# An inverse square root seeded on ScalarE by logarithm and exponential, in a windowed-attention transformer

## The reference

```
qkv = shift(x) @ Wqkv                  # 128 -> 3 * 1024
q = q / max(||q||, 1e-12) * q_scale    # per head; the same for k
q, k = rotary(q), rotary(k)            # with a growing / falling scale
sim = 8 * q k^T  in a window of 32 and the one before it
x = softmax(sim) v @ Wo + x
xn = (x' - mean) / sqrt(var + 1e-5) * g + b     # x' = shift(x)
a, gate = split(xn @ W1 + b1)
x = a * gelu(gate) @ W2 + b2 + x
```

## Time and profile before

| | |
|---|---|
| median of 3 runs | 1795.9 us (1795.12 to 1799.96) |
| the profiled execution | 1795.17 us, span 1793.4 us |
| mean granted TensorE clock | 0.965 |
| busy: PE / DVE / ACT / POOL | 1619.5 / 1467.1 / 1106.4 / 992.7 us |

### The profile page before, as it was taken

How to read it: one execution, slowest core, us unless ns; L and a number is a source line. 1 busy time by engine, 2 the same in 40 slices (tenths; PEclk the granted TensorE clock), 3 DMA queues, 4 the chain that set the end, 5 groups by cost and what they waited for, 6 DMA issues and landing times. The chain is left out here.

```text
span 1793.4 us, 75405 instructions
## 1 busy us (share of the span) xinstructions
PE 1619.5 (90%) x31917; PEld 1247.0 (70%) x32013; DVE 1467.1 (82%) x3193; ACT 1106.4 (62%) x1990; POOL 992.7 (55%) x952
## 2 busy tenths in 40 slices
PE   5369999899999889999989999999999989999985
PEld 2147777677777767777767777767777767777762
DVE  8768888888888888888888888888888788888852
ACT  5236666566666656666656666666666656666652
POOL 2246646665555666555666546676556485565420
PEclk8579999999999999999999999999999999999998
DMA  3011111211101210111111111111101111011101
GB/s 100 26 51 36 39 28 31 77 32 36 50 24 36 61 46 27 47 36 36 56 42 38 47 36 35 52 46 39 47 24 39 59 47 39 24 47 39 36 14 48
DMA packets 40597, 74.95 MB, mean 42 GB/s; under 512 B 8992, under 2 KB 22088, under 8 KB 40264
## 3 DMA queue, kind: packets, MB, share of 16 engines
q1 hardware_dynamic: 40264, 70.11, 13.3%
HBM read 20.08 MB, written 2.10 MB: 12 GB/s over the span
## 5 line engine op out<-in xcount | busy, mean ns | idle before, releaser
L773 POOL TENSOR_TENSOR qk<-qk,qk_sin 128x512 f32<-128x512 f32 x384 | 490.9, 1278 | 217.0 <-DVE qk_sin L847 217.0
L781 POOL TENSOR_TENSOR qk<-qk,rnorm 128x512 f32<-128x512 f32 x384 | 400.4, 1043 | 371.7 <-DVE rnorm L884 371.7
L1024 ACT ACTIVATE squares<-bank 128x512 f32<-128x512 f32 x384 | 228.9, 596 | 168.2 <-DVE qk_sin L847 166.5
L1150 PE MATMUL bank<-w_hi,xs_hi 128*128 128x512 f32 x576 | 290.9, 505 | 14.0 <-ACT squares L1024 7.9
L857 DVE TENSOR_REDUCE norm<-squares 128x8 f32<-128x512 f32 x384 | 258.2, 677 | 30.7 <-ACT squares L1024 28.5
L841 DVE TENSOR_TENSOR qk<-bank,tables 128x512 f32<-128x512 f32 x384 | 261.5, 681 | 6.8 <-PE bank L1152 5.8
L847 DVE TENSOR_TENSOR qk_sin<-bank,tables 128x512 f32<-128x512 f32 x384 | 261.1, 680 | 0.0
L1160 PE MATMUL bank<-ident,qk 128*128 128x128 f32 x1536 | 236.5, 277 | 5.8 <-POOL qk L781 5.1
L1152 PE MATMUL bank<-w_hi,xs_lo 128*128 128x512 f32 x576 | 229.7, 399 | 0.0
L1151 PE MATMUL bank<-w_lo,xs_hi 128*128 128x512 f32 x576 | 228.3, 396 | 0.0
L1160 PEld LDWEIGHTS bank<-ident,qk 128*128 128x128 f32 x1536 | 184.8, 141 | 54.5 <-POOL qk L781 5.9
(11 more groups left out here) (161 smaller groups left out, 2588.1 us busy)
## 6 DMA issues: line engine op xcount, KB each, us to landing
v<-v SPq DMA_DIRECT2D x96, 390.0 KB, 3.5
v<-v SPq DMA_DIRECT2D x72, 130.0 KB, 3.4
w_raw<-in_L_ffn_Wqkv SPq DMA_DIRECT2D x36, 256.0 KB, 3.2
w_o_s<-in_L_ffn_Wo SPq DMA_DIRECT2D x6, 512.0 KB, 5.2
w_s<-in_L_ffn_W SPq DMA_DIRECT2D x6, 341.0 KB, 4.8
mix_x_nat<-in_L_attn_x SPq DMA_DIRECT2D x4, 256.0 KB, 3.7
x_res_scratch<-mix_x_res SPq DMA_DIRECT2D x4, 256.0 KB, 2.7
f_x_res<-x_res_scratch SPq DMA_DIRECT2D x4, 256.0 KB, 3.5
```

Of the source, the lines that this page charges most:

```text
L773: pool.tensor_tensor(qk[:, g % 2, c, :], qk[:, g % 2, c, :], qk_sin[:, c, :], ALU.add).then_inc(added[c], 1)
L781: pool.tensor_tensor(view, view, rnorm[:, g % 2, c * HPC:(c + 1) * HPC].unsqueeze(2) .to_broadcast([P, HPC, DH]), ALU.mult).then_inc(norme ...
L1024: act.activation(squares[:, c % 2, :], bank_of(Q0 + c)[:], ACT.Square).then_inc(squared[c], 1)
L1150: pe.matmul(bank_of(c)[:], l_hi, w_hi[:, cols], start=True, stop=False)
```

## The change

The clamp becomes a function of its own and moves to the end of the step before. ScalarE computes the seed as exp(-0.5 ln n) in two activations at the end of its step, and DVE does one Newton round of three instructions. Explicit loads bring in set number 6, which holds both functions: one at the start, one after the third Gelu of an item (t = 1), and one ahead of the seed at t = 0, behind the first Gelu.

```
+            def clamp(g):
+                if not rooted_block(g):
+                    return
+                x = norm2[:, root_columns(g)]
                 if live(g):
                     for c in range(QK_CHUNKS):
                         dve.wait_ge(summed[c], g + 1)
-                    need(dve, normed[1], g - 1)
-                if with_var:
-                    dve.wait_ge(var_taken, item)
-                seq(dve.tensor_scalar(x, x, 1e-24, None, ALU.max))
-                seq(dve.tensor_scalar(y.bitcast(I32), x.bitcast(I32), -0.5, float(0x5F3759DF), ALU.mult, ALU.add))
-                seq(dve.tensor_tensor(s, x, y, ALU.mult))
+                if g % NBLK == NBLK - 1 and real(g // NBLK - 1):
+                    dve.wait_ge(var_taken, g // NBLK)
+                dve.tensor_scalar(x, x, 1e-24, None, ALU.max).then_inc(clamped, 1)
+
+            def root(g):
...
+                dve.wait_ge(seeded, root_count(g))
+                seq(dve.scalar_tensor_tensor(s, x, -0.5, y, ALU.mult, ALU.mult))
                 seq(dve.tensor_tensor(w, s, y, ALU.mult))
-                seq(dve.scalar_tensor_tensor(s, w, -10.0 / 3.0, w, ALU.add, ALU.mult))
-                seq(dve.scalar_tensor_tensor(y, s, 5.0, y, ALU.add, ALU.mult))
-                seq(dve.tensor_tensor(s, x, y, ALU.mult))
-                seq(dve.scalar_tensor_tensor(w, s, -27.0 / 1024.0, y, ALU.mult, ALU.mult))
-                dve.scalar_tensor_tensor(y, w, 9.0 / 16.0, y, ALU.add, ALU.mult).then_inc(rooted, 1)
+                dve.scalar_tensor_tensor(y, w, 1.5, y, ALU.add, ALU.mult).then_inc(rooted, 1)
...
                 sum_squares(step, 3)
+                clamp(step)
                 normalise(step - 2, 0)
...
+            def load_exp_and_log():
+                act.add_instruction(mybir.InstLoadActFuncSet(
+                    name=nc.get_next_instruction_name(), act_func_set_id=EXP_AND_LOG, engine=act.engine, ins=[], outs=[]))
+
+            def seed_root(g):
...
+                act.wait_ge(clamped, root_count(g))
+                if live(g):
+                    need(act, normed[1], g - 1)
+                act.activation(log_n[:, cols], norm2[:, cols], ACT.Ln).then_inc(logged, 1)
+                act.wait_ge(logged, root_count(g))
+                act.activation(rnorm[:, g % 2, cols], log_n[:, cols], ACT.Exp, scale=-0.5).then_inc(seeded, 1)
+
+            load_exp_and_log()
             act.wait_ge(constants_ready, N_CONST)
...
                 if t == 1:
                     gelu(item - 2, 2)
+                    if real(item - 2):
+                        load_exp_and_log()
                 take_qk(step - 2, 1)
...
                 take_v(step, 1)
+                if t == 0 and real(item - 2):
+                    load_exp_and_log()
+                seed_root(step)
```

More of the change, by code:

```diff
@@ L640, in transformer @@
     N_CONST = 5
+    EXP_AND_LOG = 6
     with ExitStack() as ctx:
@@ L656, in transformer @@
         squares = sb("squares", [P, 2, CHUNK])
-        norm2, root_t, root_w = (sb(name, [P, NORMS + NBLK]) for name in ("norm2", "root_t", "root_w"))
+        norm2, root_t, root_w, log_n = (sb(name, [P, NORMS + NBLK]) for name in ("norm2", "root_t", "root_w", "log_n"))
         rnorm = sb("rnorm", [P, 2, NORMS + NBLK])
@@ L683, in transformer @@
         rotated, summed, rooted = sems("rotated", 4), sems("summed", 4), sem("rooted")
+        clamped, logged, seeded = sem("clamped"), sem("logged"), sem("seeded")
         maxed, shifted, inverted, o_normed = sems("maxed", 2), sems("shifted", 2), sems("inverted", 2), sems("o_normed", 2)
@@ L710, in root_count, with rooted_block @@
             return g + 1 if live(g) else BLOCKS + 1
+        def rooted_block(g):
+            return live(g) or g % NBLK == NBLK - 1 and 0 <= g // NBLK - 1 < ITEMS
         def bank_of(c):
@@ L859, in sum_squares, with root_columns @@
                                   AX.X, ALU.add).then_inc(summed[c], 1)
-            def root(g):
+            def root_columns(g):
                 item, t = divmod(g, NBLK)
                 with_var = t == NBLK - 1 and real(item - 1)
-                if not live(g) and not with_var:
+                return slice(0 if live(g) else NORMS, NORMS + NBLK if with_var else NORMS)
+            def clamp(g):
+                if not rooted_block(g):
                     return
-                cols = slice(0 if live(g) else NORMS, NORMS + NBLK if with_var else NORMS)
-                x, y = norm2[:, cols], rnorm[:, g % 2, cols]
-                s, w = root_t[:, cols], root_w[:, cols]
+                x = norm2[:, root_columns(g)]
                 if live(g):
@@ L872, in root @@
                         dve.wait_ge(summed[c], g + 1)
-                    need(dve, normed[1], g - 1)
-                if with_var:
-                    dve.wait_ge(var_taken, item)
-                seq(dve.tensor_scalar(x, x, 1e-24, None, ALU.max))
-                seq(dve.tensor_scalar(y.bitcast(I32), x.bitcast(I32), -0.5, float(0x5F3759DF), ALU.mult, ALU.add))
-                seq(dve.tensor_tensor(s, x, y, ALU.mult))
-                seq(dve.tensor_tensor(w, s, y, ALU.mult))
-                seq(dve.scalar_tensor_tensor(s, w, -10.0 / 3.0, w, ALU.add, ALU.mult))
-                seq(dve.scalar_tensor_tensor(y, s, 5.0, y, ALU.add, ALU.mult))
-                seq(dve.tensor_tensor(s, x, y, ALU.mult))
-                seq(dve.scalar_tensor_tensor(w, s, -27.0 / 1024.0, y, ALU.mult, ALU.mult))
-                dve.scalar_tensor_tensor(y, w, 9.0 / 16.0, y, ALU.add, ALU.mult).then_inc(rooted, 1)
+                if g % NBLK == NBLK - 1 and real(g // NBLK - 1):
+                    dve.wait_ge(var_taken, g // NBLK)
+                dve.tensor_scalar(x, x, 1e-24, None, ALU.max).then_inc(clamped, 1)
+            def root(g):
+                if not rooted_block(g):
+                    return
+                cols = root_columns(g)
+                x, y = norm2[:, cols], rnorm[:, g % 2, cols]
+                s, w = root_t[:, cols], root_w[:, cols]
+                dve.wait_ge(seeded, root_count(g))
+                seq(dve.scalar_tensor_tensor(s, x, -0.5, y, ALU.mult, ALU.mult))
+                seq(dve.tensor_tensor(w, s, y, ALU.mult))
+                dve.scalar_tensor_tensor(y, w, 1.5, y, ALU.add, ALU.mult).then_inc(rooted, 1)
             def maximum(g, r):
@@ L1088, in gelu @@
                                bias=vecs[0:n, B1_GATE + j, layer_of(m):layer_of(m) + 1]).then_inc(gelu_done, 1)
+            def load_exp_and_log():
+                act.add_instruction(mybir.InstLoadActFuncSet(
+                    name=nc.get_next_instruction_name(), act_func_set_id=EXP_AND_LOG, engine=act.engine, ins=[], outs=[]))
+            def seed_root(g):
+                if not rooted_block(g):
+                    return
+                item, t = divmod(g, NBLK)
+                with_var = t == NBLK - 1 and real(item - 1)
+                cols = slice(0 if live(g) else NORMS, NORMS + NBLK if with_var else NORMS)
+                act.wait_ge(clamped, root_count(g))
[5 more added lines that the diff above has]
+            load_exp_and_log()
             act.wait_ge(constants_ready, N_CONST)
```

## The result

The changed kernel takes 1829.03 us in the median of four runs (1825.63 to 1833.94), the kernel before 1795.51 us (1791.16 to 1799.96). The ratio is 1.0189, with a 95% interval of 1.0153 to 1.0225: 1.9% slower. The profiled execution has a span of 1825.3 us and a mean granted clock of 0.970, against 1793.4 us and 0.965 (from 200 to 1700 us it is 1.00, and 0.99 before), so the clock isn't the reason. The time was added in the loop: the last block's projection of V1 starts at 1744.98 us and not at 1712.36, 32.6 us later.

The account below looks back on a forecast made before the run. The prediction took TensorE (PE), busy 1423.9 of 1500 us, as what bounds the kernel. Its terms, 33.9 + 8.4 + 8.4 - 14.5 - 1.8 = +34.4 us, gave 1830 us, 1.9% slower, range 1808 to 1852.

Parts of the forecast that it names:

- What VectorE's chain is worth: DVE's root chain: 112 us less busy time, worth nothing in nearly all steps because PE doesn't wait for it.
- The wait at t = 1, +33.9: Seed and two table loads delay the second Gelu; PE waits 1.54 us at expand in 22 items.
- The load behind the third Gelu: Explicit load at t = 1 ahead of take_qk: costs nothing, with 0.3 us left before the scores.
- The 0.4 us at t = 2 and t = 3, +8.4 each: Seeds ending t = 1 and t = 2 delay the v copy; PE's Q1 projection waits 0.38 us, 22 times each.
- End of t = 3, nothing: Seed's 0.56 us before the next t = 0 lies in the v copy's 1.00 us wait for PE: no cost.
- Changes of layer, -14.5: PE's root wait and slow stretch vanish at five layer changes; 2.9 us kept each, after POOL gives some back.
- The end, -1.8: Two rnorm waits of 2.1 us at the end shrink by 1.15 and 0.6 us.
- the one on the clock: Rival: granted clock falls in each new t = 1 wait, 26 us more, 1856 us; chance 0.12.
- PE's own stalls would take the waits in: Rival: issue stalls (49.3 us) ahead of the scores absorb the whole +34.4 us, giving 1795 us; chance 0.05.
- VectorE paces the loop: Rival: 1.15 us less per step becomes a gain, 1734 us; chance 0.08 with all smaller gains.
- The drain beside each load: Rival: ACT stands still 1.28 us beside each new table load, 56 us more, 1886 us; chance 0.02.

Follow-up runs that it names:

- e2: Kernel before with one round in VectorE's chain (five instructions, not nine; coarse roots), nothing on ScalarE: 1781.44 us, ratio 0.9906.
- e1: Changed kernel with Identity in place of Gelu and no explicit loads inside the loop, seeds kept: 1787.23 us, ratio to the kernel before 0.9933.
- e8: Changed kernel, but the t = 0 block keeps VectorE's chain of nine and the load ahead of its seed goes: 1794.59 us, ratio to kernel before 0.9978.
- e6: Kernel before with one unused 128x1 Exp at the end of each t = 0 step, forcing the table switches: 1828.14 us, ratio 1.0186.
- e5: Changed kernel with an unread 128x1024 copy on ScalarE ahead of the load at t = 0: 1869.02 us, ratio to the kernel before 1.0401.
- e4: Changed kernel with only the t = 3 block seeded on ScalarE, others on the chain of nine, no load at t = 0: 1788.19 us, ratio to kernel before 0.9937.
- e3: Changed kernel with one more table load written ahead of the seed at t = 0; trace still had 98 loads: 1830.45 us, ratio to kernel before 1.0166.

## Why the prediction was right

The forecast was 1830 us, from a sum of +34.4; the medians differ by 33.5 us and the spans by 31.9. The mechanism is the one forecast, and its term makes up nearly the whole. That the total came within 1 us is in part luck: over 22 items the wait at t = 1 brought 2 us more than forecast, the steps with t = 2 and t = 3 some 6 us less, and the end gave back 1 us less.

- **What VectorE's chain is worth.** Right. It is worth nothing in ordinary items (e2), and DVE's busy time fell by 98 us, where I had 112. The four that are left take 230 ns in the mean (200 to 248), as I had it, but the nine took 221 and not 231: the one row that I took for all was among the dearest. That makes 104 us; the other 6 weren't looked for.
- **The wait at t = 1, +33.9.** Right in mechanism and nearly in size: 1.63 us on the distance and not 1.54, 35.9 us in 22 items (34.2 in the items 2 to 22). The small activations take 230 ns and not 204; twice 27 ns is over half of the difference. e1 and e8 take this term away, e6 brings it about alone, e5 makes it longer.
- **The load behind the third Gelu.** Right: with two loads fewer at t = 0 and this one kept, e8 shows no growth at t = 1.
- **The 0.4 us at t = 2 and t = 3, +8.4 each.** Right in place. By the distances they are 7.6 and 11.8 us. The first was as forecast: in the changed kernel the copy of `v` ends at 1026.00, and PE starts behind it at once.

```profile
1025.42 0.58 ACT L1026 COPY v<-bank 128x512 f32<-128x512 f32 x1
...
1026.05 0.50 PE L1184 MATMUL bank<-w_hi,xs_hi 128*128 128x512 f32 x1
```

  The second was 0.43 us in ordinary items and 0.96 in the last of a layer. There the clamp takes 0.61 us and not 0.18, and Ln, which waits for it, begins 0.53 us behind the copy and not 0.10:

```profile
897.41 0.60 ACT L1026 COPY v<-bank 128x512 f32<-128x512 f32 x1
...
897.90 0.61 DVE L881 TENSOR_SCALAR norm<-norm 128x32 f32<-128x32 f32 x1
...
898.55 0.23 ACT L1114 ACTIVATE log_n<-norm 128x32 f32<-128x32 f32 x1 [0.53 <-DVE norm L881]
```

  My sum had 0.03 us for the wait for the clamp everywhere, and no row for a stretched one. Taken over whole steps, t = 2 grew by 4.1 us in the 21 items, and t = 3 by 6.3 in the 16 of them that don't end a layer (the other five are counted with the changes of layer): 10.4 in all, where 42 x 0.38 us would be 16. This is where I was furthest off: I let each delay stand to the end of the loop. What gives the rest back wasn't settled; the distances behind, which hold the scores, move by 0.1 to 0.2 us in kernels without this edit too.
- **End of t = 3, nothing.** Right. The copy that waited 1.00 us now waits less, and PE goes on without a gap:

```profile
1055.39 0.59 ACT L1026 COPY v<-bank 128x512 f32<-128x512 f32 x1 [0.58 <-PE bank L1186]
```

- **Changes of layer, -14.5.** The step with t = 0 is 11.5 us shorter over the five, and the last step of a layer 3.1, so the size is right, but not made up as I had it. The gain in the last step is none that I forecast; e2, which has a short chain and no seed on ScalarE, has it too (4.5 us), and e4, whose chain in that step is the long one, has 0.5. And I said that PE would find the root done each time. In two of five it still waits (1.32 and 1.17 us). The third had its wait replaced by another one:

```profile
359.98 0.65 PE L1322 MATMUL bank<-ident,rnorm 128*128 128x128 f32 x4 [1.32 <-DVE rnorm L893]
...
1197.97 0.65 PE L1322 MATMUL bank<-ident,rnorm 128*128 128x128 f32 x4 [1.17 <-DVE rnorm L893]
```

  The two waits come from when the three Newton instructions start. I had them begin where the chain of nine began, 1.0 us before PE's step (899.14 and 900.13 in the kernel before). In the changed kernel they stand behind the clamp, the two activations and a division, and in the first of the two they begin 1.0 us behind the start of PE's step (355.89). The first two take the 1.2 us that I had as the upper bound:

```profile
356.78 1.29 POOL L136 TENSOR_TENSOR w_lo<-w_raw,w_hi 128x512 fp32r<-128x512 f32 x1
...
356.89 1.23 DVE L891 SCALAR_TENSOR_TENSOR root_t<-norm,rnorm 128x36 f32<-128x36 f32 x1
...
358.02 1.28 POOL L778 TENSOR_TENSOR qk<-qk,qk_sin 128x512 f32<-128x512 f32 x1
...
358.15 1.20 DVE L892 TENSOR_TENSOR root_w<-root_t,rnorm 128x36 f32<-128x36 f32 x1
...
359.38 0.54 DVE L893 SCALAR_TENSOR_TENSOR rnorm<-root_w,rnorm 128x36 f32<-128x36 f32 x1
```

  And this is the third change of layer:

```profile
916.35 0.60 PE L1322 MATMUL bank<-ident,rnorm 128*128 128x128 f32 x4
...
923.18 0.34 PE L1228 MATMUL bank<-k_t,q_t 64*32 64x64 f32 x13 [3.08 <-issue]
```

```profile
924.00:926.00 2.00, 2.00 (x7) 1.52 (x7) 2.00 (x4) 1.04 (x2) 2.00 (x3) 0.52 0.00 0
```

  Here the 2.66 us for `rnorm` were gone, and 3.08 us of "issue" came in the middle of the scores a little later, where the kernel before had 0.47; the clock then fell to 0.52 all the same. e4 shows 3.02 us at the same place, e2 2.55, and e6, where the wait for `rnorm` stays, no wait of 0.3 us or more. What PE waits for there the profile doesn't say. That instructions come late while the weights load is my reading, and it isn't shown.
- **The end, -1.8.** The two waits for `rnorm` fell from 1.95 and 2.04 us to 0.63 and 1.52, 1.8 us as forecast. But the time from the last projection to the end is only 0.7 us shorter.

Of the rivals, the one on the clock didn't come true, but e5 shows how near it was: 0.9 us more of waiting, and the clock fell in half of the items, for 1.7 us each time where I had 1.2. That PE's own stalls would take the waits in is ruled out, since the stalls went from 49.3 to 54.6 us. That VectorE paces the loop is ruled out by e2. The drain beside each load isn't there. In the timeline above Ln starts 0.01 us behind the load that began at 1003.44 (1004.72 to 1004.73), and Gelu 0.02 us behind the one at 1005.24; both loads start 0.02 us behind the instruction ahead of them. By the figure of the Trainium skill, "ScalarE: Activation LUTs", section "What ACT_TABLE_LOAD costs", each would have had 1380 ns more. The trace doesn't agree: with two of them the distance at t = 1 would have grown by over 4 us, and it grew by 1.63.

## What to carry to other kernels

Don't weigh an operation that moves to another engine by its busy time. Look at the place in that engine's queue: how long it stands idle there, and who waits for what comes next. Here the same 0.5 us cost nothing at the end of a step with t = 3, some 0.4 us at the end of one with t = 1 or t = 2, and 1.6 us at the end of one with t = 0, because there a table switch and its return came with it. Look also for the one piece of a change that pays, and keep that alone: the seed at t = 3 needs no new switch and makes the kernel 0.4 to 0.6% faster, where the whole change makes it 1.9% slower.

## What the runs showed of the hardware

- A wait of PE of 2.37 us was followed by a granted clock of 0.50 in some items and of 1.00 in others, at the same place of the same kernel (e5: the clock fell in 11 of 22 items). Behind 22 waits of 0.9 to 1.5 us at this place in the changed kernel it never fell. So a wait's length alone doesn't tell what the clock does.
- An explicit load of the table set in use leaves no instruction in the trace (e3: 98 loads, with 24 more written out).
- Beside GpSimd's work for the next layer a clamp of 128x32 on DVE took 0.61 us (897.90) and not 0.18, and Newton instructions of 128x36 took 1.23 and 1.20 us (356.89, 358.15). These two ended 0.05 us behind the GpSimd instruction that was under way when they began.
- An activation of 128x32 takes 230 ns, one of 128x1 203 ns (e6), and a copy of 128x54 204 ns. So the time isn't set by the columns alone.
